# A feed-forward input joined between two weight loads into another buffer, and low parts subtracted by POOL

## The chip, the core and the metric
The kernel runs on one core of a Trainium2 chip. The metric is device time in microseconds (us), here of one launch. Six engines work side by side: PE (TensorE, matrix products), DVE (VectorE), ACT (ScalarE), POOL (GpSimd) and SP (which only issues DMAs); PEld is PE's loading of weights. Each engine runs its own instructions in order and waits on semaphores. POOL and SP both issue DMAs from their instruction streams, so whatever waits in such a stream holds back everything behind it.

## The reference
A post-norm transformer layer on x of shape (4, 512, 512), 16 heads of 32, causal, and a gated feed-forward of width 2048 whose weights are stored as integers with scales:

```
qkv  = x @ w_qkv.T + b_qkv
att  = softmax(q k^T / sqrt(32) + causal) v
x    = layernorm(x + att @ w_out.T + b_out)                       # y1 in the kernel
W    = (int_weight - 128) * scale[:, None]                        # gate, up, down
out  = layernorm(x + (silu(x @ Wg.T) * (x @ Wu.T)) @ Wd.T)
```

## The kernel before
**Numbers in two parts.** Activations go through PE as a high part (rounded to fp32r, written by ACT) and a low part (the whole minus the high part). For an input x they are xT_hi and xT_lo, transposed, [128, 4, 512] each; chunk c is xT[:, c, :].

**Attention.** 16 groups G, four per batch b (G = 4b + g), one group for four heads; each has 16 steps s. PE's order within a group is written by hand (`filling`, `TASK_STEPS`, `PRODUCT_STEPS`): scores of the next group, transposes of the probabilities (L1323), products with the values (L1344), and between them projections, 12 matmuls each. In group g = 2 PE does two output projections of the batch before ("o", drained by DVE at L1040) and then q and k of the next batch, from step 8. In group 15 there is little filling: PE's step 15 is the transposition of the inverse row sums (L1355), which waits for POOL's `widen_inverse(15)`.

**Inputs of later batches.** `turn(n)` transposes 16-bit halves of the input by DMA into x_tok, `store_halves`/`load_halves` bring them round through HBM, and `join(n)` on POOL (L680, four copies) puts the halves together. For n <= 4 the whole goes to x_whole, which lies on the same bytes as xT_lo; for n > 4 to yT_next. Here n = 1 to 3 are attention inputs, n = 4 to 7 the inputs of FFN batches 0 to 3. In group g = 2 ACT makes xT_hi of the next batch (`next_hi`, L790) and DVE, in place, xT_lo (`next_lo`, L981), at the steps X_STEPS or X_FIRST (group 2).

**POOL in groups 14 and 15.** join(4), att_lo(13), add_bias(3) (L694: the bias added to the last batch's residual in scan_buf), widen_inverse(14), the norm of batch 2 (L655); then att_lo(14), store_third (DMAs that store y1 of batch 2), choose_path (a flag that says whether the weights are exact in bf16), widen_inverse(15), att_lo(15), the norm of batch 3.

**Feed-forward.** `ffn`, `first_batch` and `ffn_batch`: FFN batches 0 to 3, each of 16 blocks i. PE does 8 gate and 8 up matmuls (L1451 with xT_hi, L1452 with xT_lo), and up to 8 down matmuls of the block before (L1458, L1459). ACT applies silu (L896) and makes hid_hi (L902), DVE multiplies (L1118) and makes hid_lo (L1122). In batch 0 ACT also widens the bf16 weights that SP's DMA transposes bring (`load_short`; 12 DMAs a chunk). Two paths are compiled; with these inputs the short one runs. POOL's loop over PIECES nevertheless issues its 48 loads of integer weights into the two buffers of w_int (L752), each waiting for the one two before, and `join(5)` follows it. `root` (L648, the power for the norm) and joins 6 and 7 come after.

**From one FFN batch to the next.** After the last up product ACT makes xT_hi from yT_next (`y_hi`, L909) and DVE xT_lo (`y_lo`, L1127), and PE's first gate products wait for them one chunk at a time. The residual y1 of the finished batch is loaded into z_tok (r_loaded); `finish` on DVE does one step after each block of the next batch from i = 0: four residual additions with statistics, the variance, four norms. SP then stores the four outputs, loads the next residual and the next halves. At the end of batch 0 SP's queue is: last chunk's transposes (L553 to L559), the four stores of y1 of batch 3 (L536), a wait for third_stored and for y1_stored = 16·3·4, the residual load (L608), then `turn(6)`.

Of the kernel before, what the change touches and what calls it, by code (L numbers as in the profile page):

```python
# [6 lines left out]
def postln_block_kernel(nc: bass.Bass, x, w_qkv, b_qkv, w_out, b_out, gate_w, gate_scale, up_w, up_scale,  # L7
# [9 lines left out]
    F32, F32R, I32, U32 = mybir.dt.float32, mybir.dt.float32r, mybir.dt.int32, mybir.dt.uint32  # L17
# [46 lines left out]
    PRODUCT_STEPS = [8, 8, STEPS, STEPS, STEPS, STEPS]  # L64
    INVERSE_STEP = 15
    SLOTS = 7
    X_STEPS = [1, 2, 5, 6]
    X_FIRST = [3, 5, 6, 7]


# [47 lines left out]
    def x_at(G, s):  # L118
        return [c for c in range(ND) if (X_STEPS if G > NG else X_FIRST)[c] == s] if G % NG == 2 else []

# [103 lines left out]

    SHORT_PIECES = FIRST_PIECES + [p for i in range(NI) for p in pieces_at(i, True)]
    INTS = 2
    HIDS = NT


# [13 lines left out]
    with ctx:  # L243
# [221 lines left out]
        def evict_task(eng, G, i, copy):  # L465
            wait_full(eng, "t", G, i)
            copy(probsT[:, (G * BLOCKS + i) % SLOTS, :], bank_of("t", G, i)[:, :]).then_inc(drained_of("t", G, i), 1)  # L467

        def residual(b):
            return scan_buf if b == LAST else z_tok  # L470

# [8 lines left out]
        def _(sp):  # L480
# [122 lines left out]
                sp.wait_ge(*piece_evicted(("d", 0, t), SHORT_PIECES))  # L603
            load_short(3)
            store_y1(B - 1)
            sp.wait_ge(third_stored, 16 * NT)
            sp.wait_ge(y1_stored, 16 * (B - 1) * NT)
            sp.dma_start(z_tok[:, :, :], y1_v[0]).then_inc(r_loaded, 16)  # L608

            def store_out(b):  # L610
# [21 lines left out]
        def _(pool):  # L632
# [32 lines left out]
            def join(n):  # L665

                pool.wait_ge(halves_loaded, 16 * n)
                if n <= B:
                    wait_full(pool, "k", NG * n - 1)
                    out = x_whole  # L670
                else:
                    out = yT_next
                    if n == B + 1:

                        for kind in range(3):
                            pool.wait_ge(staged[kind][2], 16 * ND)
                    else:
                        pool.wait_ge(yT_done, ND * (n - B - 1))
                for c in range(ND):
                    nc.gpsimd.tensor_copy(out[:, c, :].bitcast(U16).rearrange("p (s h) -> p s h", h=2),  # L680
                                          halves[:, c, :, :].rearrange("p h s -> p s h")).then_inc(joined, 1)

            def widen_inverse(G):

# [35 lines left out]
            for G in range(GROUPS):  # L720
                b, g = divmod(G, NG)
                if g == 2:
                    join(b + 1)
                if G > 0:
                    att_lo(G - 1)
                if g == 2 and b == LAST:
                    add_bias(LAST)
                if G == GROUPS - 1:
                    store_third()
                    choose_path()  # L730
                widen_inverse(G)
                if 1 <= G <= 3 * CHUNKS:
                    shorten(G - 1)
                if g == 2 and b > 0:
                    for t in range(NT):
                        apply_norm(b - 1, t)
                if g == 0 and b > 0:
                    add_bias(b - 1)
# [4 lines left out]
            for j in range(HG):  # L743
                pool.wait_ge(score_full[j], GROUPS * PER_GROUP)
            for m in range(len(PIECES)):
                if m >= INTS:

                    pool.wait_ge(*piece_evicted(PIECES[m - INTS]))
                    pool.wait_ge(fw_loaded[m % INTS], 16 * (m // INTS))
                kind, n = PIECES[m][:2]  # L750
                src = gate_v[n] if kind == "g" else up_v[n] if kind == "u" else down_v[n, PIECES[m][2]]
                nc.gpsimd.dma_start(w_int[:, m % INTS, :], src).then_inc(fw_loaded[m % INTS], 16)  # L752
            join(B + 1)
            for b in range(B - 1):
                root(b, var2_done, rstd2_done)
                if b + 2 < B:
# [12 lines left out]
        def _(act):  # L769
# [134 lines left out]
            def y_hi(b, c):  # L904

                if c == 0:
                    act.wait_ge(up_full, (b + 1) * NI)
                act.wait_ge(joined, b * ND + (ND * B + c + 1))
                nc.scalar.activation(xT_hi[:, c, :], yT_next[:, c, :], ACT.Copy).then_inc(yT_hi_done, 1)  # L909

            def first_batch(weights):
                for n in range(len(FIRST_PIECES)):
# [46 lines left out]
        def _(dve):  # L959
# [18 lines left out]
            def next_lo(n, c):  # L978

                dve.wait_ge(x_hi_done, NT + ND * (n - 1) + c + 1)  # L980
                nc.vector.tensor_tensor(xT_lo[:, c, :], x_whole[:, c, :], xT_hi[:, c, :].bitcast(F32),  # L981
                                        ALU.subtract).then_inc(xT_done, 1)
# [94 lines left out]
            for G in range(GROUPS):  # L1077
                b, g = divmod(G, NG)
                if G == GROUPS - 1:
                    dve.wait_ge(scanned, LOADS * PER_SCAN)  # L1080
                    nc.vector.tensor_reduce(scan_rows[:, :], scan_sums[:, :], mybir.AxisListType.X, ALU.max).then_inc(scan_rows_done, 1)
                for s in range(STEPS):
                    for job in ENDED.get(G * STEPS + s, []):
                        take(job)
                    if s in MAX_STEPS:
                        ahead, qb, heads = MAX_STEPS[s]
                        for j in heads if G + ahead < GROUPS else ():
                            tile_max(G + ahead, qb, j)
                    for i in tasks_at(s):
                        if i % 2 == 1:  # L1090
                            evict_task(dve, G, i, nc.vector.tensor_copy)
                    if s == 1 and G > 0:
                        normalise(G - 1)
                    if s == 2:
                        inverse_sum(G, 0)
                    if s == 9:
                        inverse_sum(G, 1)
                    for c in x_at(G, s):
                        next_lo(b + 1, c)
                    if (G, s) in W_STEPS:  # L1100
                        w_lo(W_STEPS[G, s])
                    for job in ENDED.get(G * STEPS + s, []):
                        if job[0] == "o":
                            output_statistics(*job[1:])
                    if g == 2 and s == 9 and b > 0:
                        variance(b - 1, mv_done, var_done)
# [17 lines left out]
            def y_lo(b):  # L1124
                for c in range(ND):
                    dve.wait_ge(yT_hi_done, b * ND + c + 1)
                    nc.vector.tensor_tensor(xT_lo[:, c, :], yT_next[:, c, :], xT_hi[:, c, :].bitcast(F32),  # L1127
                                            ALU.subtract).then_inc(yT_done, 1)

            def drain_down(b, t):  # L1130
# [30 lines left out]
            def ffn_batch(b, ahead):  # L1161
                steps = finish(b - 1)
                for i in range(NI):
                    hidden(b, i, up_acc[i % 2])
                    next(steps, None)
                if ahead:
                    y_lo(b)
                    for t in range(NT):
                        drain_down(b, t)
# [411 lines left out]
```

## Time and profile before
| | us |
|---|---|
| three runs, median | 775.86 (772.34 to 777.63) |
| the profiled execution | 770.71 |
| its span, first to last instruction | 768.6 |
| PE busy | 715.2 (93%) |
| DVE busy | 398.3 (52%) |
| ACT busy | 374.6 (49%) |
| POOL busy | 167.9 (22%) |
| chain that ended last | PE 84%, DVE 6%, DMA 4%, ACT 3%, POOL 1% |

Busy time is that of the profiled execution. Matmuls overlap, so that a busy PE need not be PE at its peak: the distance between the starts of two equal matmuls says more than how long one lasts. The attention ends at about 379.8 us of the span and the four FFN batches fill the rest.

### The profile page before, as it was taken

To read this page: it belongs to the slowest core of one execution; us is meant where nothing else is said; L and a number is where in the kernel's file an instruction comes from. 1 tells how busy PE (TensorE), PEld (TensorE's weight loads), DVE (VectorE), ACT (ScalarE), POOL (GpSimd) and SP (SyncE) were. 2 spreads that over 40 slices of the span, in tenths; PEclk is the share of its full clock that TensorE was granted. 3 is DMA by queue.
4 is the path that set the end of the run, shared out by engine and by line. 5 is a ranking of instruction groups with operands and counts; after the bars stand their busy time and mean duration, and the time that the engine had idled before them with its cause. 6 is when DMAs were issued, how large, how long until landed. Compare 5 with 4: busy or idle time off the path is not lost.

```text
span 768.6 us, 11736 instructions
## 1 busy us (share of the span) xinstructions
PE 715.2 (93%) x4368; PEld 554.5 (72%) x4368; DVE 398.3 (52%) x1004; ACT 374.6 (49%) x900; POOL 167.9 (22%) x182
## 2 busy tenths in 40 slices
PE   7998899999999999997999993299999999999995
PEld 6776577776777777775888882188888888888884
DVE  4766766776666866678433220353326432463335
ACT  3665776676666866677565540122223222322230
POOL 0000312226132440338262223300010002000003
PEclk9999999999999999999999997599999999999998
DMA  8701654246733483324979745430340013000201
GB/s 309 199 14 29 138 139 136 70 110 157 242 84 67 99 245 112 84 78 102 226 152 202 241 141 150 115 90 28 136 105 6 0 45 119 0 1 28 82 1 56
DMA packets 97207, 83.35 MB, mean 108 GB/s; under 512 B 64128, under 2 KB 73344, under 8 KB 97024
## 3 DMA queue, kind: packets, MB, share of 16 engines
q1 hardware_dynamic: 90624, 62.69, 28.5%
q0 software_dynamic: 6528, 19.93, 11.3%
q8 instruction: 34, 0.56, 0.3%
q14 instruction: 21, 0.17, 0.1%
HBM read 59.53 MB, written 22.02 MB: 106 GB/s over the span
## 4 chain that ended last, share of the span: by engine, by line
PE 84%; DVE 6%; DMA 4%; ACT 3%; issue 1%; POOL 1%; SPq 0%; POOLq 0%; DVEq 0%; ACTq 0%
PE bank L1451 15%; PE bank L1452 15%; PE bank L1244 11%; PE bank L1323 9%; PE bank L1459 7%; PE bank L1458 7%; PE bank L1262 6%; PE bank L1306 5%; PE bank L1344 5%; PE bank L1281 4%; DVE probs L1002 2%; ACT probs L795 2%; DMA w_int<-in_L_ffn_up_w_dram 2%; DMA w_int<-in_L_ffn_down_w_dram 1%; DVE xT_lo L981 1%
## 5 line engine op out<-in xcount | busy, mean ns | idle before, releaser
L795 ACT ACTIVATE probs<-probs,neg_max 128x128 f32<-128x128 f32 (+3 forms) x256 | 140.4, 552 | 6.9 <-DVE neg_max L1002 6.9
L1002 DVE CUSTOM_DVE_ANT_0 probs<-bank,causal 128x128 f32<-128x128 f32 (+3 forms) x256 | 111.7, 483 | 40.2 <-PE bank L1306 40.2
L1118 DVE SCALAR_TENSOR_TENSOR hid<-bank,u_scale,silu 128x512 f32<-128x512 f32 x64 | 48.0, 750 | 160.7 <-PE bank L1452 159.6
L1451 PE MATMUL bank<-xT_hi,gateT 128*128 128x512 f32 x256 | 100.7, 393 | 27.5 <-DVE xT_lo L1127 27.5
L1452 PE MATMUL bank<-xT_lo,gateT 128*128 128x512 f32 x256 | 100.5, 393 | 0.0
L1323 PEld LDWEIGHTS bank<-ident,probs 128*128 128x128 f32 x640 | 71.2, 140 | 40.5 <-issue 25.7
L1451 PE MATMUL bank<-xT_hi,upT 128*128 128x512 f32 x256 | 100.1, 391 | 0.0
L1452 PE MATMUL bank<-xT_lo,upT 128*128 128x512 f32 x256 | 100.1, 391 | 0.0
L1323 PE MATMUL bank<-ident,probs 128*128 128x128 f32 x640 | 88.3, 277 | 6.7 <-DVE probsT L467 5.3
L847 ACT ACTIVATE probsT<-bank 128x512 f32<-128x512 f32 x80 | 47.7, 597 | 96.0 <-PE bank L1323 94.5
L896 ACT ACTIVATE silu<-bank,g_scale 128x512 f32<-128x512 f32 x64 | 44.0, 687 | 103.5 <-PE bank L1452 103.5
L1458 PE MATMUL bank<-downT,hid_hi 128*128 128x512 f32 x232 | 90.3, 389 | 0.5 <-DVE hid_lo L1122 0.5
L1459 PE MATMUL bank<-downT,hid_lo 128*128 128x512 f32 x232 | 90.3, 389 | 0.0
L902 ACT ACTIVATE hid_hi<-hid 128x512 fp32r<-128x512 f32 x58 | 36.7, 632 | 109.7 <-DVE hid L1118 109.7
L1451 PEld LDWEIGHTS bank<-xT_hi,gateT 128*128 128x128 f32 x256 | 48.6, 190 | 38.0 <-DVE xT_lo L1127 27.9
L467 DVE COPY probsT<-bank 128x512 f32<-128x512 f32 x80 | 54.8, 686 | 26.2 <-PE bank L1323 26.1
L1122 DVE TENSOR_TENSOR hid_lo<-hid,hid_hi 128x512 fp32r<-128x512 f32 x58 | 40.1, 692 | 40.5 <-ACT hid_hi L902 40.5
L1452 PEld LDWEIGHTS bank<-xT_lo,gateT 128*128 128x128 f32 x256 | 48.6, 190 | 10.1
L1451 PEld LDWEIGHTS bank<-xT_hi,upT 128*128 128x128 f32 x256 | 48.5, 189 | 10.2
L1452 PEld LDWEIGHTS bank<-xT_lo,upT 128*128 128x128 f32 x256 | 48.3, 189 | 10.1
L1244 PE MATMUL bank<-xT_hi,wT_hi 128*128 128x512 f32 x128 | 54.4, 433 | 0.3 <-DVE xT_lo L975 0.2
L1306 PE MATMUL bank<-k_sb,q_sb 32*128 32x512 f32 (+3 forms) x512 | 48.1, 467 | 3.3 <-DVE neg_max L1002 3.2
(102 smaller groups left out, 1156.7 us busy)
## 6 DMA issues: line engine op xcount, KB each, us to landing
halves<-x_tok SPq DMA_DIRECT2D x7, 1024.0 KB, 6.7
x_tok<-halves SPq DMA_DIRECT2D x7, 1024.0 KB, 7.9
scan_buf<-in_L_ffn_gate_w_dram SPq DMA_DIRECT2D x4, 1024.0 KB, 5.3
scan_buf<-in_L_ffn_up_w_dram SPq DMA_DIRECT2D x4, 1024.0 KB, 5.6
scan_buf<-in_L_ffn_down_w_dram SPq DMA_DIRECT2D x4, 1024.0 KB, 5.0
w_int<-in_L_ffn_gate_w_dram POOLq DMA_DIRECT2D x16, 256.0 KB, 3.0
w_int<-in_L_ffn_up_w_dram POOLq DMA_DIRECT2D x16, 256.0 KB, 2.9
w_int<-in_L_ffn_down_w_dram POOLq DMA_DIRECT2D x16, 256.0 KB, 3.6
```

Of the source, the lines that this page charges most:

```text
L467: copy(probsT[:, (G * BLOCKS + i) % SLOTS, :], bank_of("t", G, i)[:, :]).then_inc(drained_of("t", G, i), 1)
L795: nc.scalar.activation(probs[qb][:, j, :], probs[qb][:, j, :], ACT.Exp, bias=neg_max[:, qb, j:j + 1], scale=-1.0, accum_out=row_sum[:, qb, ...
L847: evict_task(act, G, i, lambda o, i: nc.scalar.activation(o, i, ACT.Copy))
L1002: nc.vector.tensor_tensor_reduce(out=probs[qb][:, j, :], in0=score[j][:, first:first + w], in1=causal[:, S - w:S], scale=-SCALE, scalar=-F ...
L1118: nc.vector.scalar_tensor_tensor(out=hid[:, i % 2, :], in0=bank[:, :], scalar=u_scale[:, i:i + 1], in1=silu[:, i % 2, :], op0=ALU.mult, op ...
L1244: last = nc.tensor.matmul(acc[:, :], w[:, c, e], xT[:, c, :], start=at == 0, stop=at == MM - 1)
L1306: last = nc.tensor.matmul(score[j][:, first:first + w], q_sb[G % 2][rows, qb * P:(qb + 1) * P], k_sb[G % 2][rows, 0:w], start=True, stop=True)
L1323: last = nc.tensor.transpose(acc[:, m * P:(m + 1) * P], probs[qb][:, j, kb * P:(kb + 1) * P], ident[:, :])
L1451: nc.tensor.matmul(acc[n][:, :], w[:, c, cols], form(xT_hi[:, c, :]), start=c == 0, stop=False)
L1452: last = nc.tensor.matmul(acc[n][:, :], w[:, c, cols], form(xT_lo[:, c, :]), start=False, stop=c == ND - 1)
L1458: nc.tensor.matmul(down_acc[t][:, :], form(hi[:, tok]), w_down[:, i, :], start=i == 0, stop=False)
L1459: return nc.tensor.matmul(down_acc[t][:, :], form(lo[:, tok]), w_down[:, i, :], start=False, stop=i == NI - 1)
```

## The change
join(5) moves from behind the loop over PIECES to ahead of its load m = 16 (JOIN_AT). It writes z_tok instead of yT_next and waits until y1 of all batches that SP stores has been stored; `y_hi(0)` and `y_lo(0)` read z_tok (`y_whole`). Its old wait for the transposed chunk 2 (which lies on memory of yT_next) goes to join(6). SP's residual load of batch 0 waits for y_lo(0) instead of the stores. `finish` starts at i = 2 in each batch.

For batches 2 and 3 and FFN batch 0 (groups 6, 10 and 14) the twelve subtractions of `next_lo` are done by POOL, two before and two after att_lo; ACT's next_hi moves from steps 1, 2, 5, 6 to 1, 2, 3, 4. Group 2 keeps DVE's. add_bias(3) moves from group 14 to group 15, ahead of store_third.

```diff
@@ -64,7 +64,7 @@
     PRODUCT_STEPS = [8, 8, STEPS, STEPS, STEPS, STEPS]
     INVERSE_STEP = 15
     SLOTS = 7
-    X_STEPS = [1, 2, 5, 6]
+    X_STEPS = [1, 2, 3, 4]
     X_FIRST = [3, 5, 6, 7]
 
 
@@ -224,6 +224,8 @@
 
     SHORT_PIECES = FIRST_PIECES + [p for i in range(NI) for p in pieces_at(i, True)]
     INTS = 2
+
+    JOIN_AT = 16
     HIDS = NT
 
 
@@ -466,6 +468,9 @@
             wait_full(eng, "t", G, i)
             copy(probsT[:, (G * BLOCKS + i) % SLOTS, :], bank_of("t", G, i)[:, :]).then_inc(drained_of("t", G, i), 1)
 
+        def y_whole(b):
+            return z_tok if isinstance(b, int) and b == 0 else yT_next
+
         def residual(b):
             return scan_buf if b == LAST else z_tok
 
@@ -603,8 +608,7 @@
                 sp.wait_ge(*piece_evicted(("d", 0, t), SHORT_PIECES))
             load_short(3)
             store_y1(B - 1)
-            sp.wait_ge(third_stored, 16 * NT)
-            sp.wait_ge(y1_stored, 16 * (B - 1) * NT)
+            sp.wait_ge(yT_done, ND)
             sp.dma_start(z_tok[:, :, :], y1_v[0]).then_inc(r_loaded, 16)
 
             def store_out(b):
@@ -668,9 +672,12 @@
                 if n <= B:
                     wait_full(pool, "k", NG * n - 1)
                     out = x_whole
+                elif n == B + 1:
+                    pool.wait_ge(y1_stored, 16 * NT * LAST)
+                    out = z_tok
                 else:
                     out = yT_next
-                    if n == B + 1:
+                    if n == B + 2:
 
                         for kind in range(3):
                             pool.wait_ge(staged[kind][2], 16 * ND)
@@ -679,6 +686,11 @@
                 for c in range(ND):
                     nc.gpsimd.tensor_copy(out[:, c, :].bitcast(U16).rearrange("p (s h) -> p s h", h=2),
                                           halves[:, c, :, :].rearrange("p h s -> p s h")).then_inc(joined, 1)
+
+            def next_lo(n, c):
+                pool.wait_ge(x_hi_done, NT + ND * (n - 1) + c + 1)
+                nc.gpsimd.tensor_tensor(xT_lo[:, c, :], x_whole[:, c, :], xT_hi[:, c, :].bitcast(F32),
+                                        ALU.subtract).then_inc(xT_done, 1)
 
             def widen_inverse(G):
 
@@ -721,11 +733,16 @@
                 b, g = divmod(G, NG)
                 if g == 2:
                     join(b + 1)
+                    if b > 0:
+                        next_lo(b + 1, 0)
+                        next_lo(b + 1, 1)
                 if G > 0:
                     att_lo(G - 1)
-                if g == 2 and b == LAST:
+                if g == 2 and b > 0:
+                    next_lo(b + 1, 2)
+                    next_lo(b + 1, 3)
+                if G == GROUPS - 1:
                     add_bias(LAST)
-                if G == GROUPS - 1:
                     store_third()
                     choose_path()
                 widen_inverse(G)
@@ -743,6 +760,8 @@
             for j in range(HG):
                 pool.wait_ge(score_full[j], GROUPS * PER_GROUP)
             for m in range(len(PIECES)):
+                if m == JOIN_AT:
+                    join(B + 1)
                 if m >= INTS:
 
                     pool.wait_ge(*piece_evicted(PIECES[m - INTS]))
@@ -750,7 +769,6 @@
                 kind, n = PIECES[m][:2]
                 src = gate_v[n] if kind == "g" else up_v[n] if kind == "u" else down_v[n, PIECES[m][2]]
                 nc.gpsimd.dma_start(w_int[:, m % INTS, :], src).then_inc(fw_loaded[m % INTS], 16)
-            join(B + 1)
             for b in range(B - 1):
                 root(b, var2_done, rstd2_done)
                 if b + 2 < B:
@@ -906,7 +924,7 @@
                 if c == 0:
                     act.wait_ge(up_full, (b + 1) * NI)
                 act.wait_ge(joined, b * ND + (ND * B + c + 1))
-                nc.scalar.activation(xT_hi[:, c, :], yT_next[:, c, :], ACT.Copy).then_inc(yT_hi_done, 1)
+                nc.scalar.activation(xT_hi[:, c, :], y_whole(b)[:, c, :], ACT.Copy).then_inc(yT_hi_done, 1)
 
             def first_batch(weights):
                 for n in range(len(FIRST_PIECES)):
@@ -1095,8 +1113,8 @@
                         inverse_sum(G, 0)
                     if s == 9:
                         inverse_sum(G, 1)
-                    for c in x_at(G, s):
-                        next_lo(b + 1, c)
+                    for c in x_at(G, s) if b == 0 else ():
+                        next_lo(1, c)
                     if (G, s) in W_STEPS:
                         w_lo(W_STEPS[G, s])
                     for job in ENDED.get(G * STEPS + s, []):
@@ -1124,7 +1142,7 @@
             def y_lo(b):
                 for c in range(ND):
                     dve.wait_ge(yT_hi_done, b * ND + c + 1)
-                    nc.vector.tensor_tensor(xT_lo[:, c, :], yT_next[:, c, :], xT_hi[:, c, :].bitcast(F32),
+                    nc.vector.tensor_tensor(xT_lo[:, c, :], y_whole(b)[:, c, :], xT_hi[:, c, :].bitcast(F32),
                                             ALU.subtract).then_inc(yT_done, 1)
 
             def drain_down(b, t):
@@ -1162,7 +1180,8 @@
                 steps = finish(b - 1)
                 for i in range(NI):
                     hidden(b, i, up_acc[i % 2])
-                    next(steps, None)
+                    if i >= 2:
+                        next(steps, None)
                 if ahead:
                     y_lo(b)
                     for t in range(NT):
```

## Rows read from the trace of the kernel before

**Rows 1.** The page: granted PE clock in 40 slices of the span
```profile
PEclk9999999999999999999999997599999999999998
```

**Rows 2.** Waits: engine, line, waited for: us in total, times, longest
```profile
PE bank L1451 <- DVE xT_lo L1127: 27.5, 1, 27.5
```

**Rows 3.** Timeline of PE, FFN boundaries: start us, us, engine, line, operation [idle before]
```profile
467.36 0.40 PE L1459 MATMUL bank<-downT,hid_lo 128*128 128x512 f32 x1
495.21 0.79 PE L1451 MATMUL bank<-xT_hi,gateT 128*128 128x512 f32 x1 [27.45 <-DVE xT_lo L1127]
495.80 0.63 PE L1452 MATMUL bank<-xT_lo,gateT 128*128 128x512 f32 x1
...
584.87 0.39 PE L1451 MATMUL bank<-xT_hi,gateT 128*128 128x512 f32 x1
...
671.91 0.39 PE L1451 MATMUL bank<-xT_hi,gateT 128*128 128x512 f32 x1
```

**Rows 4.** Timeline of POOL, weight loads 16 and 48 and join(5)
```profile
428.45 0.54 POOL L752 DMA_DIRECT2D w_int<-in_L_ffn_up_w_dram  x1 [2.28 <-ACT upT L871]
...
489.66 0.54 POOL L752 DMA_DIRECT2D w_int<-in_L_ffn_up_w_dram  x1 [1.35 <-DMA w_int<-in_L_ffn_up_w_dram]
490.19 4.41 POOL L680 COPY yT_next<-x_tok 128x1024 uint16<-128x1024 uint16 x4
```

**Rows 5.** Timeline of SP's queue; DMA issues: KB each, median us to landing
```profile
424.60 2.94 SPq L536 DMA_DIRECT2D y_scratch<-z_tok  x4
432.29 0.39 SPq L608 DMA_DIRECT2D z_tok<-y_scratch  x1
...
z_tok<-y_scratch SPq DMA_DIRECT2D x4, 1024.0 KB, 5.6
```

**Rows 6.** Timelines of ACT, DVE and POOL at ends of batches 0 and 1, and batch 2
```profile
464.16 0.63 ACT L902 ACTIVATE hid_hi<-hid 128x512 fp32r<-128x512 f32 x1 [1.91 <-DVE hid L1118]
...
581.86 2.18 ACT L909 ACTIVATE xT_hi<-yT_next 128x512 fp32r<-128x512 f32 x4
...
582.60 2.49 DVE L1127 TENSOR_TENSOR xT_lo<-yT_next,xT_hi 128x512 fp32r<-128x512 f32 x4
...
610.95 1.01 POOL L648 TENSOR_TENSOR ln_rstd<-ln_var,half_power 128x4 f32<-128x4 f32 x1 [50.05 <-DVE ln_var L1024]
643.44 4.46 POOL L680 COPY yT_next<-x_tok 128x1024 uint16<-128x1024 uint16 x4 [31.49 <-DMA x_tok<-halves]
```

**Rows 7.** Starts of groups 5, 6 and 7 in the chain; PE's timeline in group 6
```profile
137.01 1.65 PE bank L1344 x32
...
158.79 1.65 PE bank L1344 x32
...
181.87 1.65 PE bank L1344 x32
...
172.19 0.50 PE L1244 MATMUL bank<-xT_hi,wT_hi 128*128 128x512 f32 x1
...
174.64 1.09 PE L1323 MATMUL bank<-ident,probs 128*128 128x128 f32 x8 [0.79 <-DVE probsT L467]
```

**Rows 8.** Timelines of DVE, PE and POOL, groups 14 and 15
```profile
346.65 2.94 DVE L981 TENSOR_TENSOR xT_lo<-x_whole,xT_hi 128x512 fp32r<-128x512 f32 x2
...
352.69 1.09 PE L1323 MATMUL bank<-ident,probs 128*128 128x128 f32 x8 [1.78 <-DVE probsT L467]
...
344.82 5.90 POOL L694 TENSOR_TENSOR scan_buf<-scan_buf,bias_o 128x512 f32<-128x512 f32 x4
353.57 0.61 POOL L686 COPY inv_wide<-inv_sum 128x512 f32<-128x512 f32 x1 [2.84 <-DVE inv_sum L1009]
...
363.59 1.29 POOL L662 TENSOR_TENSOR attT_lo<-attT,attT_hi 128x512 fp32r<-128x512 f32 x1
...
369.12 0.61 POOL L686 COPY inv_wide<-inv_sum 128x512 f32<-128x512 f32 x1 [1.38 <-DVE inv_sum L1009]
...
370.60 0.60 PE L1355 MATMUL bank<-ident,inv_wide 128*128 128x128 f32 x4
```

## The prediction

> **What bounds the kernel now.** The page's 40 slices come first: TensorE (PE) is granted its full clock nearly everywhere, with one dip two thirds of the way through [rows 1]. The list of waits puts a length on it: PE stood still once for 27.5 us at the first gate product of a feed-forward (FFN) batch, released by VectorE's (DVE's) xT_lo [rows 2]. PE's timeline places it: the last down product of FFN batch 0 is issued at 467.36, the first gate product of batch 1 at 495.21 [rows 3]. POOL's timeline says why: the sixteenth of its 48 weight loads (256 KB each, m=15) is issued at 428.45, 32 more follow, the last at 489.66, and only then does join(5) run, 490.19 to 494.60 [rows 4]. Those loads fill w_int, which the short path taken here (bf16 weights from SP's transposes) never reads; they cost nothing but POOL's order. Elsewhere PE is the bound, so a gain must come from an interval in which PE waits: this one, and smaller ones in groups 6, 10 and 14 [rows 7, 8].
>
> **The join and its new place.** It needs its halves, whose load SP issues before load_short(1), three transposed chunks ahead of the stores of rows 5, and now also y1_stored = 192, because z_tok must have been stored before the join writes it. SP waited on that same count before its residual load, issued at 432.29 [rows 5], so the count was there by then. SP's queue up to that point is unchanged: its last four stores are issued from 424.60. POOL issues m=15 at 428.45 [rows 4], waits until about 432.2 and joins in 4.41 us: finished at 436.6. The 32 loads behind it start 5 us late; nobody on this path waits for them.
>
> ACT takes y_hi(0, c) only after the last up product and hidden_hi(0, 15), which starts at 464.16 [rows 6]. The margin is 27 us. At the later boundaries y_hi takes 2.18 us for four and y_lo 2.49 [rows 6]: 0.54 and 0.62 each. So y_hi(0,0) ends near 465.3, y_lo(0,0) near 466.1, before PE has issued its last down product (467.36). One matmul's pitch is 87.04/(16 x 24) = 0.23 (the 87.04 is worked out below), so batch 1 starts at 467.59. Saved: 495.21 - 467.59 = **27.6 us**.
>
> **The clock after the stall.** The first products after it take 0.79 and 0.63 us against 0.39 [rows 3]; the slices show the lower grant there [rows 1]. From first gate product to first gate product batch 1 takes 584.87 - 495.21 = 89.66 us, batch 2 671.91 - 584.87 = 87.04. The 2.62 us are the price of starting at 1.2 instead of 2.4 GHz; with no idle time they go too: **2.6 us**.
>
> **The residual and finish.** A block i takes 87.04/16 = 5.44 us. The load of z_tok now waits for y_lo(0), is issued at about 468.1 and lands 5.6 us later (median) [rows 5]: 474. finish(0) now starts at block i=2, some 15 us into the batch (482.6): covered by 8 us. On SP's queue the same wait stands ahead of the eight transposes of turn(6), its store of halves, the output stores and load_halves(6); turn(6) still starts 26 us earlier than before, because it waited for the join.
>
> Each later finish ends two blocks later, 10.9 us in all, and with it the output stores, the next residual and load_halves, so join(7). That join ran 643.44 - 584.87 = 58.6 us into batch 2 [rows 6]; it will run at 69.5 and end at 74.0. y_hi is taken 581.86 - 495.21 - 2.6 = 84.0 us into a batch. Cover 10 us: cost 0. In the last batch the residual has still more room.
>
> root(0), POOL's 1 us of pow, sits behind the loads. 32 loads from 428.45 to 489.66 are 1.91 us each; from 436.6 that is 497.7. The variance comes at 610.95 - 584.87 = 26.1 us into a batch [rows 6], plus 10.9: 504.6. Cover 7 us: cost 0; it would take 2.13 us per load to be late at all.
>
> **Low parts on POOL, groups 6 and 10.** One group takes 158.79 - 137.01 = 21.78 us, group 6 181.87 - 158.79 = 23.08 [rows 7]; group 10 repeats it. DVE is the late one there: PE waits 0.79 us for its probsT copy [rows 7]. DVE loses four subtractions (0.6 us each); the last two stand right in front of the output drain. On POOL one costs 1.29, as attT_lo does [rows 8]; the join (4.46, as in [rows 6]), the four and att_lo are done about 4.46 + 5 x 1.29 = 10.9 us into the group if nothing waits, 11.5 with ACT's pace; PE reaches its first projection of the next batch 172.19 - 158.79 = 13.4 in [rows 7]. The gain is between the wait, 0.79, and the whole difference, 1.30. I take 1.1, twice: **2.2 us**.
>
> **Group 14 and what gives it back.** Here the two last subtractions took 2.94 us, ahead of the drain at 349.5; PE then waited 1.78 us and more for DVE [rows 8]. Without them the drain starts when PE has the bank full, near 346.6: 2.9 us earlier for DVE, and PE follows. But add_bias(3), 5.90 us between 344.82 and 350.7 in which POOL would otherwise have idled until 353.57, moves to group 15, ahead of the stores of the third batch, choose_path and widen_inverse(15). POOL was busy without a break from 353.57 to 369.12 - 1.38 = 367.74: 14.17 us. New: 353.57 - 2.9 + 14.17 + add_bias = 364.84 + 5.2 (four operations at 1.29) = 370.0, or 370.7 at 5.9. Widening takes 0.61: 370.6 to 371.3. PE's transposes of it ran at 370.60 [rows 8]. So PE arrives 2.9 us earlier, waits 2.9 us, and goes on where it did: net **0**, bounds a gain of 0.3 and a loss of 0.7. The store of the third batch lands near 373, before the drain at 378 that needs it.
>
> The 2.94 us for two subtractions stand beside POOL's add_bias, which itself took 5.90 for four operations of 1.29 [rows 8]. The Trainium skill (SBUF — State Buffer, Who interferes with whom) says that a DVE instruction with two SBUF inputs and a POOL instruction that reads SBUF block each other, not one with a single SBUF input. The trace agrees. By it POOL's twelve subtractions meet only DVE operations with one input in PSUM, and the sum stays; were it false for these, some 0.6 us more per meeting would fall on DVE.
>
> **Sum.** -27.6 - 2.6 - 2.2 + 0.1 = -32.3. The profiled execution took 770.71 us (span 768.6); it would take 738.4, with a span near 736.3. The median of the three runs shown is 775.86, 5.2 above the profiled one. I carry that over: **743.5 us**.
>
> **Rivals.**
> *The new pause in group 15 costs the clock.* PE would stand 2.9 us in one piece; the longest seen at the full clock in that stretch is 1.78 [rows 8], and after 27.5 it was gone. If it falls, 2.6 us are lost again as in batch 1: 746.1. The Trainium skill (TensorE: Matmul & The Clock Gate, The HAM clock gate) says that the array drops to 1.2 GHz after idle activity and comes back only after sustained work; the drop after the stall is there, what so short a pause does no row shows.
> *POOL's root(0) comes late.* If the loads run at 2.5 us beside turn(6), the last ends at 516.6, 12 us after the variance. DVE's apply at block 7 would stand about 6 us, of which PE, running ahead, feels 2 or 3, and the following joins shift into the 10 us cover: 746 to 749. For it: the transposes are new beside the loads. Against: the rate already contains a stretch with transposes.
> *The cover of the later joins is too thin.* If the shifted load_halves lands over 10 us later than worked out, batches 2 and 3 each wait; 5 us each gives 753.
> *Slower.* The join now depends on SP's last y1 stores, behind load_short(3), which waits for ACT's first twelve widened pieces. Any lateness of the stores past 432.3 + 26.6 = 459 costs PE one for one. It would eat the gain if they landed near 490, and be slower beyond; SP is issuing without a pause up to 424.60, so nothing points there. 5 us past it: 781.
> *No change.* Only if PE's wait passes to something else at the same place, such as the residual coming after y_lo: 773.7 with only groups 6 and 10. The 8 us of cover speak against it.
>
> **Chances.** The forecast 0.78, the clock rival 0.10, root(0) 0.05, thin cover 0.03, no change 0.02, slower 0.02. Without a gain from groups 6, 10 and their like the forecast's case ends at 746; with PE keeping group 14's 2.9 us it is 740.6. The three runs shown spread by 2.7 around their middle; so 738.5 to 749, which takes in the first two rivals. 1% is 7.8 us, about what a measurement here can tell from none: faster 0.95, same 0.03, slower 0.02.
>
> **What the profile will show.** PE's wait on xT_lo at the gate products gone; join(5) near 432 to 437 and m=16 behind it; the clock row without the dip; first gate products 87.0 apart in all batches; groups 6 and 10 near 22; PE waiting near 3 us for POOL's inv_wide in group 15; the group of loads ending near 498 and ln_rstd near 504, less 2 for the attention. A wait of PE or DVE on r_loaded, ln_rstd or xT_hi in batches 1 to 3 would make the prediction wrong.

## The result and the profile after

| | before | after |
|---|---|---|
| timed median (range, executions) | 774.18 us (772.34 to 777.63, 4) | 738.87 us (737.66 to 739.15, 4) |
| the profiled execution | 770.71 | 738.95 |
| its span | 768.6 | 737.1 |
| PE busy | 715.2 (93%) | 713.8 (97%) |

The kernel is faster: ratio 0.9536, 95% interval 0.9495 to 0.9577. The forecast was 743.5 us, in a range from 738.5 to 749; its change was -32.3 us on the profiled execution. The profiled executions differ by 31.8 us, the timed medians by 35.3. So the forecast time is 4.6 us too high. The median of 738.87 stands at the very low end of the range, and the ratio times the median of before (0.9536 x 774.18 = 738.3) just below it. One execution of k4, a kernel further down, ran at a mean granted clock of 0.557 and took 1195 us; it is left out of k4's median.

PE's timeline of the kernel after at the end of FFN batch 0 and the start of batch 2 (start us, us, engine, line, operation, idle before) answers to [rows 3]:

```profile
464.49 0.47 PE L1477 MATMUL bank<-downT,hid_hi 128*128 128x512 f32 x1 [0.52 <-DVE hid_lo L1140]
...
466.16 0.39 PE L1478 MATMUL bank<-downT,hid_lo 128*128 128x512 f32 x1
466.39 0.39 PE L1470 MATMUL bank<-xT_hi,gateT 128*128 128x512 f32 x1
466.62 0.39 PE L1471 MATMUL bank<-xT_lo,gateT 128*128 128x512 f32 x1
...
553.43 0.39 PE L1470 MATMUL bank<-xT_hi,gateT 128*128 128x512 f32 x1
```

The last down product and the first gate product stand 0.23 us apart, where 495.21 - 467.36 = 27.85 lay between them, and the first products last 0.39 instead of 0.79. Batch 1 takes 553.43 - 466.39 = 87.04. The join is where the reader of the diff looks for it; POOL's timeline of after, then SP's:

```profile
429.68 0.54 POOL L771 DMA_DIRECT2D w_int<-in_L_ffn_up_w_dram  x1 [1.63 <-DMA w_int<-in_L_ffn_down_w_dram]
431.22 4.80 POOL L687 COPY z_tok<-x_tok 128x1024 uint16<-128x1024 uint16 x4 [1.00 <-DMA y_scratch<-z_tok]
435.97 0.54 POOL L771 DMA_DIRECT2D w_int<-in_L_ffn_down_w_dram  x1
...
500.83 0.54 POOL L771 DMA_DIRECT2D w_int<-in_L_ffn_up_w_dram  x1 [2.36 <-DMA w_int<-in_L_ffn_up_w_dram]
503.35 1.04 POOL L652 TENSOR_TENSOR ln_rstd<-ln_var,half_power 128x4 f32<-128x4 f32 x1 [1.98 <-DVE ln_var L1042]
536.93 3.37 POOL L687 COPY yT_next<-x_tok 128x1024 uint16<-128x1024 uint16 x3 [32.54 <-DMA x_tok<-halves]
...
623.04 4.46 POOL L687 COPY yT_next<-x_tok 128x1024 uint16<-128x1024 uint16 x4 [31.64 <-DMA x_tok<-halves]
```

```profile
466.79 0.39 SPq L612 DMA_DIRECT2D z_tok<-y_scratch  x1
467.28 11.83 SPq L524 DMA_TRANSPOSE x_tok<-y_scratch  x8
```

The join waits 1.00 us for the stores of y1 and no longer. The last load is issued at 500.83, and root(0) at 503.35 waited only for its variance, the last 1.98 us of it with the loads done. SP issues the residual load at 466.79 and the transposes right behind it. join(6) runs 536.93 - 466.39 = 70.5 us into batch 1, join(7) 623.04 - 553.43 = 69.6 us into batch 2.

What is left are short waits of PE. Its list of after (engine, line, waited for: us in total, times, longest), against [rows 2]:

```profile
...
PE bank L1325 <- DVE neg_max L1020: 3.2, 2, 2.2
PE bank L1374 <- POOL inv_wide L698: 2.7, 1, 2.7
PE bank L1342 <- DVE probsT L469: 1.2, 2, 1.0
```

The second of these three is new. It is group 15's, and something follows it. PE's timeline of after, then its windows (us, then each engine's busy time, the granted clock, DMA share, GB/s):

```profile
367.81 0.63 PE L1374 MATMUL bank<-ident,inv_wide 128*128 128x128 f32 x4 [2.67 <-POOL inv_wide L698]
368.37 2.80 PE L1363 MATMUL bank<-probsT,v_tok 128*32 128x256 f32 x32
371.09 0.80 PE L1300 MATMUL bank<-wT_hi,attT_hi 128*128 128x512 f32 x1
371.69 0.63 PE L1300 MATMUL bank<-wT_lo,attT_hi 128*128 128x512 f32 x1
...
372.43 0.39 PE L1300 MATMUL bank<-wT_hi,attT_hi 128*128 128x512 f32 x1
```

```profile
367.00:368.00 1.00, 0.19 (x2) 0.22 (x3) 0.00 (x0) 0.00 (x0) 0.67 (x2) 1.00 1.00 354
368.00:369.00 1.00, 1.00 (x16) 0.66 (x18) 0.00 (x0) 0.53 (x1) 0.00 (x0) 0.93 1.00 346
369.00:370.00 1.00, 1.00 (x15) 0.43 (x9) 0.00 (x0) 0.98 (x2) 0.00 (x0) 0.50 1.05 347
...
372.00:373.00 1.00, 1.00 (x5) 0.77 (x5) 0.00 (x0) 0.73 (x2) 0.28 (x1) 0.87 0.93 24
```

Behind the pause PE runs at 1.2 GHz (0.50) for some 3.4 us: the 32 products take 2.80 us, not the 1.65 to 1.72 they take elsewhere.

**Where the time went.** PE's timelines of both profiled executions, cut at the same instructions (the 32 products with the values at the starts of groups 3 and 14, then the first gate product of each batch):

| stretch | before | after | change | forecast |
|---|---|---|---|---|
| start to group 3 | 93.28 | 93.13 | -0.15 | 0 |
| to group 14 (6 and 10 within) | 242.46 | 239.91 | -2.55 | -2.2 |
| group 14 to first gate product | 44.02 | 45.55 | +1.53 | +0.1 |
| FFN batch 0, with the stall | 115.45 | 87.80 | -27.65 | -27.6 |
| batch 1 | 89.66 | 87.04 | -2.62 | -2.6 |
| batch 2 | 87.04 | 87.04 | 0 | 0 |
| batch 3 and tail | 96.69 | 96.63 | -0.06 | 0 |
| span | 768.6 | 737.1 | -31.5 | -32.3 |

In the third stretch group 14 is 2.93 us shorter (20.53 to 17.60) and group 15, up to its products with the values, 2.87 longer, of it the wait of 2.67. From those products to the first gate product it is 1.59 us more (8.63 to 10.22): the low clock, as k4 confirms below.

### The profile page after: what moved, and what is told of

Same layout as the page of the kernel before. It is cut to its first block, busy times and chain, and to the rows that moved or that the text cites. A ratio compares the mean times of both kernels' runs of the same rounds, so it can differ in the third digit from the quotient of the medians.

```text
span 737.1 us, 11735 instructions
## 1 busy us (share of the span) xinstructions
PE 713.8 (97%) x4368; PEld 554.3 (75%) x4368; DVE 388.5 (53%) x992; ACT 373.6 (51%) x900; POOL 182.7 (25%) x194
## 4 chain that ended last, share of the span: by engine, by line
PE 91%; POOL 3%; DVE 3%; ACT 1%; issue 1%; DMA 0%; POOLq 0%; DVEq 0%
PE bank L1471 16%; PE bank L1470 16%; PE bank L1263 12%; PE bank L1342 9%; PE bank L1477 7%; PE bank L1478 7%; PE bank L1281 6%; PE bank L1325 6%; PE bank L1300 5%; PE bank L1363 5%; POOL z_tok L659 1%; PE bank L1229 1%; PE bank L1374 1%; DVE probs L1020 1%; POOL scan_buf L706 1%; POOL z_tok L783 1%
```

## The experiments

Every kernel below stands on a base in which the 104 transposing DMAs (the 16-bit halves and the bf16 weights) are plain copies of the same number of bytes, cut into 128 x 128 blocks; the halves are taken from the gate weights. So its result isn't the reference's, and it is compared with the base kernels, i1 and i2, stretch by stretch. Stretches are named as in the table above: A, B, C, then D0 and D1 for batches 0 and 1.

**i1, i2: the base kernels.**

> The kernel before with one thing left out, so that its output isn't the reference's: the 104 transposing DMAs of SP are plain copies of the same bytes in 256-byte pieces (those of turn read the gate weights instead of x or y1, so that all numbers stay finite). All engine work, waits and other DMAs stand. It is the base of the experiments. Both theories of the scatter (L: the weight loads in front of join(5); S: spread over the kernel) need the stall of PE on DVE xT_lo to be here: 15 to 28 us, shorter than 27.5 because the DMA engines have less to do beside the loads; span 755 to 769. Theory L: this span less that wait is the 741.1 of before within 2. Theory S gives no such tie.

> The changed kernel with the same replacement of the transposing DMAs. No wait of PE on xT_lo, span 737.1 within 1, PE waiting 2.7 us for inv_wide in group 15 and its clock at half for some 4 us after. Theory L: its runs agree within 1.5 us and those of the base before scatter by several; theory S: both scatter alike.

Measured: 768.74 us (766.06 to 771.18, 6 executions) and 738.69 (737.80 to 741.63, 4). The profiles give A 95.47, B 242.33, C 44.61, D0 111.27, D1 89.23 for i1, and 94.53, 239.85, 45.50, D0 89.06, D1 87.05 for i2. The change does in the base what it does in the original, with a stall some 4 us shorter (23.28 us). i2's profiled span of 739.7 misses the 737.1 expected: A is 1.4 us longer than in the kernel after, and D0 1.3, with a new wait of PE of 0.95 us for hid_lo at 431.77. j3 and k4 have that D0 too, the others of this form 87.83; why isn't shown. Theory L, that the scatter lies in the loads ahead of the join alone, fails: the executions of i2, without a stall, are 3.8 us apart and not 1.5, against 5.1 in i1. The span less the wait, by that theory 741.1 within 2, is 743.3 in i1, 742.7 in n1 and 743.8 in n3.

**j1, j2: one part each.** j1 takes the attention's part back (DVE subtracts, add_bias(3) in group 14), j2 the join's (place, buffer, waits and finish). Cuts of the edits:

```diff
# j1, in the kernel after
-    X_STEPS = [1, 2, 3, 4]
+    X_STEPS = [1, 2, 5, 6]
...
-                    for c in x_at(G, s) if b == 0 else ():
-                        next_lo(1, c)
+                    for c in x_at(G, s):
+                        next_lo(b + 1, c)
# j2, in the kernel after
-                if m == JOIN_AT:
-                    join(B + 1)
...
+            join(B + 1)
```

> Base kernels throughout: the 104 transposing DMAs replaced by plain copies. The join's part of the change alone (join(5) ahead of load 16 into z_tok, residual load after y_lo(0), finish from i=2); low parts and add_bias as before. By the prediction's terms: base before in its profile 766.6 us of span, of it 23.3 of stall and 2.6 of slow clock: 740.7, PE with no wait on xT_lo. Theory L (the scatter of the timed runs of before, 766.1 to 771.2 in the base, lies in the loads ahead of join(5)): these runs agree within 1.5 us. Theory S (it lies all over the kernel): they scatter by 5.

> Base with the attention's part alone (POOL's low parts, ACT's steps, add_bias(3) in group 15); join(5) behind all 48 loads as before. The attention ends about 1.2 us earlier (2.5 from groups 6 and 10, 2.9 from 14, less 2.7 of wait for inv_wide and 1.6 of slow clock). The end of the stall is set by POOL, which starts its loads 1.2 us earlier: the kernel gains 0 to 2 us, not more, and PE's wait on xT_lo stays 22 to 25 us. Theory L and theory S: runs scatter by several us, since the loads are still in front of the join.

Measured: j1 742.69 (741.26 to 743.09), 26.1 below i1; no wait on xT_lo; D0 87.83, D1 87.05, B 242.38. j2 763.88 (763.31 to 764.79), 4.9 below i1, more than the 0 to 2 expected; B 239.83, C 45.53, D0 110.89. Its list of waits:

```profile
PE bank L1467 <- DVE xT_lo L1143: 22.9, 1, 22.9
...
PE bank L1371 <- POOL inv_wide L697: 2.6, 1, 2.6
```

The large part is the join's, alone; with the join in its new place the attention's part is worth another 4.0 us by the medians (i2 against j1). In j2 it shows as 2.5 us in B, less 0.9 in C. A, outside the edit, is 1.8 us shorter than in i1 (93.63 against 95.47), where group 2 ran at the low clock for longer. All of this comes through the stall. POOL's first load is issued 14.87 us behind the FFN's first product in both, so it comes 3.4 us earlier in j2 (393.86 against 397.28), and the last 3.8 us earlier. POOL's timeline of i1, then of j2:

```profile
488.14 0.54 POOL L753 DMA_DIRECT2D w_int<-in_L_ffn_up_w_dram  x1 [1.43 <-DMA w_int<-in_L_ffn_up_w_dram]
```

```profile
484.34 0.54 POOL L768 DMA_DIRECT2D w_int<-in_L_ffn_up_w_dram  x1 [1.42 <-DMA w_int<-in_L_ffn_up_w_dram]
```

**j4: the loads left out.** The kernel before with its join still behind the loop, but only the first 2 of the 48 weight loads issued (the path taken doesn't read them), and without the loop's wait for the load two before.

```diff
-                    pool.wait_ge(fw_loaded[m % INTS], 16 * (m // INTS))
...
-                nc.gpsimd.dma_start(w_int[:, m % INTS, :], src).then_inc(fw_loaded[m % INTS], 16)
+                if m < 2:
+                    nc.gpsimd.dma_start(w_int[:, m % INTS, :], src).then_inc(fw_loaded[m % INTS], 16)
```

> Base before, with 46 of POOL's 48 weight loads left out (the executed path does not read them); join(5) stays behind the loop, in yT_next, low parts on DVE. If the stall is nothing but POOL's order behind the loads, it is gone: 740.7 of span. If something else holds the join (its halves, chunk 2 in stage), a stall stays. Theory L: runs within 1.5 us of each other; theory S: a scatter of 5 us.

Measured: 740.05 (737.51 to 741.11). POOL's timeline shows the join 39 us earlier than in i1 (488.67), and D0 is 87.83:

```profile
449.90 4.47 POOL L681 COPY yT_next<-x_tok 128x1024 uint16<-128x1024 uint16 x4 [54.35 <-ACT upT L872]
```

With the join in the same place and buffer, and with its own waits, the stall is gone: it was the loads ahead of the join. That it was their order and not their traffic follows with j1, which issues all 48 and has no stall either. The executions are 3.6 us apart without any loads in the way. The profiled one, a span of 735.5 where 740.7 was expected, is 2.5 us below the median; its granted clock stays at 1.00 up to the tail.

**k1, k2: where the cover ends.** `JOIN_AT` 32 and 40 in the kernel after.

> Base after (738.7 us median, profile span 739.7) with join(5) ahead of load 32 instead of load 16. In the base's trace the loads around 31 are issued at 457.6; less the join's 4.5 us the join starts near 453 and ends near 457.5, and y_hi(0) needs its first chunk at 465.5. Theory T (the join costs PE one for one only past a point, near 464 in this trace): no wait on xT_lo, the base's time within 1 us. Rival: any later join costs something, 5 us or more.

> Base after with join(5) ahead of load 40. The join starts near 469 and ends near 473.5; chunk by chunk y_hi, y_lo and PE follow it, so that PE waits about 5 to 7 us in all on xT_lo at the first gate products: 744 to 746, 1 or 2 us more if the clock falls in the pause. Rival (the stall of before was the loads' DMA traffic, not the order): no wait.

Measured: k1 739.12 (738.37 to 739.78), as i2; k2 750.00 (746.84 to 751.42), 11.3 more than i2, and 4 to 6 over the 744 to 746 expected (2 over, if the clock's 1 or 2 us are counted in). POOL's timeline of k1, then of k2 with PE's wait:

```profile
454.82 4.46 POOL L688 COPY z_tok<-x_tok 128x1024 uint16<-128x1024 uint16 x4
```

```profile
471.06 4.41 POOL L688 COPY z_tok<-x_tok 128x1024 uint16<-128x1024 uint16 x4
...
PE bank L1471 <- DVE xT_lo L1146: 9.7, 1, 9.7
```

A join at 454.8 costs nothing and one at 471.1 stops PE: D0 is 97.71, 9.9 over batch 0 without a stall, and D1 89.63, 2.6 over. So a 9.7 us pause costs the 2.6 us of slow clock that the 27.5 us one cost. The margin argued for the join (27 us) is real: 16 loads of it can be given away.

**k3: the pause filled.** 250 identity transposes in front of batch 1's first gate product, in the kernel before: PE has to wait as long, but isn't idle.

```diff
                 down(0, NI - 1)
+                for _ in range(250):
+                    nc.tensor.transpose(gate_acc[0][:, 0:P], ident[:, :], ident[:, :])
```

> Base before (768.7 us median) plus 250 transposes of the identity on PE, 27 us of work whose result nobody reads, in front of batch 1's first gate product, where PE waits for xT_lo. They separate the stall from the clock. If the slow products after the stall come from PE having been idle: granted clock 1.00 there, batch 1 as long as batch 2 (87.0 instead of 89.7), 2.6 us shorter. If the dummies outlast the stall of 23 us, up to 4 us are lost again: then the first gate product is late by just that, and its clock is still 1.00.

Measured: 770.57 (768.25 to 772.66), not shorter: the transposes outlast the join by some microseconds (D0 115.04 against 111.27). But D1 is 87.15 and the granted clock 1.00, where i1 has 89.23: what batch 1 has over 87.04 is the clock behind an idle engine. It is 2.0 to 3.0 us in the six other profiles with a stall of 22.9 to 27.5 us (before, i1, j2, n1, n2, n3).

**j3, k4: group 15's pause.** j3 puts add_bias(3) behind widen_inverse(15); k4 leaves it and puts 22 identity transposes into the pause.

```diff
# j3, in the kernel after
-                if G == GROUPS - 1:
-                    add_bias(LAST)
...
                 widen_inverse(G)
+                if G == GROUPS - 1:
+                    add_bias(LAST)
# k4, in the kernel after
+                for _ in range(22 if G == GROUPS - 1 else 0):
+                    nc.tensor.transpose(acc[:, 0:P], ident[:, :], ident[:, :])
                 pe.wait_ge(inv_widened, G + 1)
```

> Base of the changed kernel with add_bias(3) moved behind widen_inverse(15), still ahead of att_lo(15). Theory W: the 2.7 us wait of PE for inv_wide and the half clock after it come from these four operations alone. Then the wait is gone, the granted clock is 1.00 from group 14 to the FFN, and the kernel is 2.7 + 1.6 = 4.3 us shorter than the base after (738.7): 734.4. Rival: the row sums of group 15 or att_lo(15) are as late by then, and PE waits elsewhere: 0 to 2 us.

> Base after plus 22 transposes of the identity on PE (2.4 us) in group 15 ahead of the wait for inv_wide. Theory C: of the 4.3 us that add_bias(3) costs there, 2.7 are the wait and 1.6 the slow clock after it. Then PE goes on at the same moment, at full clock, and 1.6 us are saved: 737.1 against 738.7. Rival: the clock falls for another reason (the engines' load together): no gain.

Measured: j3 735.20 (734.29 to 736.66), 3.5 below i2; C is 41.09 against 45.50. The profile of k4 gives C as 43.84, with no low clock behind the transposes:

```profile
367.22 2.56 PE L1374 MATMUL bank<-ident 128*128 128x128 f32 x22
369.97 0.66 PE L1377 MATMUL bank<-ident,inv_wide 128*128 128x128 f32 x4 [0.19 <-POOL inv_wide L699]
370.56 1.72 PE L1364 MATMUL bank<-probsT,v_tok 128*32 128x256 f32 x32
```

So of the 4.4 us that add_bias(3) costs where the change puts it, 1.7 are clock and 2.7 the wait, as the expectation had it. By the clock alone k4 should have been timed 1.7 us below i2 and wasn't: 740.83 (739.22 to 741.61, 3 executions). Its profile has 0.8 us more than i2's in A, outside the edit. The split rests on the profiles; the timing doesn't show it.

**m1: j3, with group 2's pause filled too.**

```diff
# j3 and, in group 2 at step 8, before the scores
+                            for _ in range(18):
+                                nc.tensor.transpose(spare[:, 0:P], ident[:, :], ident[:, :])
```

> The kernel with add_bias(3) behind widen_inverse(15) (735.2 us) plus 18 transposes of the identity on PE (2 us, nobody reads them) in group 2 ahead of the scores that wait 2.2 us for DVE's neg_max. In every profile but those of before and of the kernel without loads the clock fell at 82 us, behind that pause, and group 2 took 23.2 to 25.3 us instead of 23.1. Theory P (a pause of about 2 us costs the clock in some executions and not in others, and that is part of the scatter): no dip there, group 2 takes 23.1, runs lie 0.6 to 1 us lower and closer together: 734.4. Rival: no change.

Measured: 735.58 (734.64 to 737.63), the same as j3; the profile's span is 732.7, the shortest of all, with no low clock ahead of the tail and group 2 at 23.11 us. Group 2's dip costs too little there for the timing to show. Of these versions j3 is the one to take: one moved call puts it below both base kernels. With the original's transposing DMAs it wasn't tried.

**m2: finish from block 0 again** (`if i >= 2:` taken out).

> Base after with finish starting at block 0 of each batch again. The residual load is issued after y_lo(0) and lands 5 to 7 us later, when DVE has done block 0's product (3.8 us into the batch). DVE then waits about 3 us for r_loaded in batch 1 only, which its slack to PE covers: the time of the base, 738.7 within 1 us, and joins 6 and 7 start 10.9 us earlier. Rival (the wait reaches PE, which is what starting at block 2 is for): 2 to 4 us slower, with a pause of PE on hid near 475.

Measured: 739.14 (738.74 to 739.49), as i2. DVE's timeline shows the residual just late and DVE alone waiting for it:

```profile
472.86 0.69 DVE L1156 TENSOR_TENSOR z_tok<-d_scaled,z_tok 128x512 f32<-128x512 f32 x1 [0.27 <-DMA z_tok<-y_scratch]
```

The load lands 5.8 us after 467; the delay by two blocks costs nothing and is worth nothing here.

**n1, n2, n3: what differs between executions.** n1 and n3 are i1 again, n2 is i1 with group 2's 18 transposes.

> The base before once more, for its spread between executions and a second profile. Both theories: median 768.7 within 1.5. Theory C (low-clock dips after short pauses carry the offset between timed and profiled executions): wherever this profile shows a granted clock of 0.5 in groups 2 or 14, that group is 0.6 to 2.2 us longer than 23.1 or 20.5. Theory S (the length of the stall carries it): groups as in the profiled before, and the distance of the first gate products of batches 0 and 1 differs by over 1 us from the 111.27 of the first base run.

> The base before with 18 identity transposes on TensorE in the pause of group 2, as in m1_later_and_fill2. Theory C: no low clock in group 2, which takes 23.1 us; mean granted clock of the timed runs up from 0.975 by 0.003 or more, median 1 to 2 us below n1_before_again. Theory S: median within 0.5 us of n1_before_again, since the stall is the same.

> A third profile of the base before. Theory C: group 2 takes either about 23.1 us (clock full) or 24.5 to 25.5 (clock halved for 3 to 9 us), group 14 either 20.3 to 20.6 or 21.1 to 22.3. Theory S: the distance of the first gate products of batches 0 and 1 moves by over 1 us between the three profiles while groups 2 and 14 stay.

Measured: n1 769.97 (769.69 to 771.89), n2 769.01 (766.49 to 769.48), n3 770.34. From the profiles:

| | group 2 | group 14 | FFN starts | 48 loads, first to last | batch 1 starts | span |
|---|---|---|---|---|---|---|
| before, the original | 23.08 | 20.53 | 379.76 | 95.04 | 495.21 | 768.6 |
| i1 | 25.04 | 21.13 | 382.41 | 90.86 | 493.68 | 766.6 |
| n1 | 23.69 | 21.82 | 382.01 | 92.66 | 495.10 | 767.8 |
| n3 | 23.09 | 21.82 | 382.25 | 92.07 | 494.73 | 768.3 |
| n2 | 23.11 | 21.37 | 380.39 | 92.76 | 493.57 | 767.4 |
| j2 | 23.49 | 17.60 | 378.99 | 90.48 | 489.88 | 763.0 |

Both things vary, so neither theory holds alone. Groups 2 and 14 grow by up to 2.0 and 1.3 us where the clock falls behind their pauses (2.19 us in group 2; 1.07 and 1.78 in group 14). The loads of one and the same base (i1, n1, n3) take 90.9 to 92.7 us. And the stall doesn't take in what was lost before it: in all six rows the first load is issued 14.9 us behind the FFN's start, and batch 1 starts 20.4 us more than the loads' time behind it. A later FFN is a later first load. n2 against n1, -0.96 us in the median, lies just under the 1 to 2 that theory C gave and above theory S's 0.5, with a granted clock of 0.977 against 0.974, and settles neither; by the profiles its FFN starts 1.62 us earlier and its batch 1 1.53.

## Why the prediction was right on the mechanism and wrong on the time

**The stall (-27.6) and its clock (-2.6): right**, -27.65 and -2.62. The join ran at 431.22 instead of 432.2 and took 4.80 instead of 4.41; j1, j4, k1 and k2 show the reason given, POOL's order, and the margin.

**Residual, finish, root, later joins: cost 0, right.** join(7) came at 69.6 us into batch 2 (worked out: 69.5), join(6) at 70.5 into batch 1. The last load was issued at 500.83 (497.7), and root(0) waited for its variance, though with 2.0 us to spare and not 7. The two rivals built on them didn't come.

**Groups 6 and 10 (-2.2): a little small.** They took 21.84 and 21.83 against 23.07 and 23.12, the upper bound of 1.3 each. Taking DVE's lateness away took away the whole difference to a group without inputs, not only the wait of 0.79 that was in view.

**Group 14 (+0.1): the pause was right and its clock was not.** Group 14 went from 20.53 to 17.60, the 2.9 us foreseen, and PE waited 2.67 us for inv_wide, near the 2.9 given; add_bias(3) took 5.01 us in its new place (worked out: 5.2). The +0.1 of the sum isn't worked out in the prediction, which has "net 0". The stretch grew by 1.53, since the work after the pause ran at 1.2 GHz for 3.4 us. That is the rival "The new pause in group 15 costs the clock", given 1 chance in 10 at 2.6 us. It came true, at 1.6 us here and 1.7 by k4. The 1.78 us given as the longest pause seen at the full clock in that stretch came from one execution: behind that same pause the clock fell in six of the eight profiles that have it. The same profile of before also had a longer one at the full clock, the 2.19 us in group 2, as only two of the fourteen other profiles with that pause have it. The Trainium skill (TensorE: Matmul & The Clock Gate, The HAM clock gate) was cited for the drop after idle activity; the trace agrees that it drops, here behind 2.67 us.

**The sum (-32.3): right**, -31.5 by the spans. Two errors partly cancel in it, which is luck: groups 6 and 10 with the stretch around them gave 0.35 more than forecast, and the stretch from group 14 on took 1.4 more.

**The step that failed is the last: "The median of the three runs shown is 775.86, 5.2 above the profiled one. I carry that over".** The term of +5.2 us measured -0.1: the sum goes from one execution's 770.71 to 738.4, the profiled execution of after took 738.95, and the median of after is 738.87. The offset isn't a property of the kernel that a change leaves alone. The profiled executions of i1 and n1 are at their medians too (768.69 and 768.74, 769.95 and 769.97), while i2's is 2.9 us above its median and j4's 2.5 below. The profiled execution of before is lower than every timed one.

What made it lower is known in part. Over 46 timed executions of before in these comparisons (771.5 to 779.9, one at a clock of 0.924 left out) the time goes with the length of low clock, 2(1 - c) times the span for a mean granted clock c: correlation 0.65, 0.44 us per us. The profiled one has c = 0.977, 35 us of low clock, the typical one 0.970 to 0.972, 43 to 46. That doesn't tell two causes apart. The profiled one's clock didn't fall in groups 2 and 14, and theirs may have; or their loads may have taken longer, which lengthens the stall and its low clock with it. Both happen in the base. j4 has no stall, and its profiled execution, the other one at full clock in both groups, is 2.5 us below its median, so the dips alone may make that much. How the original's 5.2 us divide stays open, since it has no second profile. Each of the candidates was out of place in the forecast: group 2's dip is in after's profile already, and the pauses of group 14 and the loads ahead of the join went with the change.

What could have been known: the offset had three values beside it (1.6, 5.2 and 6.9 for the three runs shown). A forecast from the profiled execution alone, with the offset as the upper end of the range, would have named 738.4, 0.5 us from the median of after. In the prediction the 5.2 stands in the forecast and in the time of each rival, and no case is worked out in which it is missing.

## What to carry to other kernels

A profile of one execution gives a difference, not a level: take the sum against the profiled time, and let the distance to the timed median be one end of the range rather than a term, above all where the change removes the stall in which executions differ. When an operation is moved off a slack engine, look at what PE waits for next on that engine's queue: one call ahead of inv_wide gave back 4.4 us, 1.7 of them through the clock, and moving it behind returned 3.5. A queue that feeds a dead path is not free if something live stands behind it; the cover is read from where the consumer would take it (here 454.8 cost nothing, 471.1 cost 11 us).

## What the runs showed of the hardware

The clock can fall behind much shorter pauses than the 27.5 us of before, and not in every execution. In the profiles of before and after, i1 to m2 and n1 to n3, the 2.67 us pause of group 15 was followed by 0.50 in all six profiles that had it idle (after, i2, j2, k1, k2, m2); group 2's 2.19 us was followed by it in 12 of the 15 that had it, for 3.4 to 6.8 us, and not in before, j4 and n3; group 14's 1.07 and 1.78 us in i1, j1, k3, n1, n2 and n3 and not in before and j4. Identity transposes in the pause kept it at 1.00 each time (k3, k4, m1, n2). A pause of 9.7 us cost 2.6 us of clock, pauses of 22.9 to 27.5 us cost 2.0 to 3.0.

That the same pause has both outcomes was not expected. The Trainium skill (TensorE: Matmul & The Clock Gate, The HAM clock gate) says that where the clock rises after a cold start varies between runs of one kernel; these profiles show it of the fall as well.

A stall that is ended by another engine's queue moves with what starts that queue. In the six profiles of the table above PE's stall ended 20.4 us plus the time of the 48 loads behind the FFN's start, whatever the clock had cost before; and that time, in one and the same program, differed by 1.8 us between three executions (90.86 to 92.66).
